# One tower of a vision transformer on one core: the class rows' product through Wo ahead of the third group's turnings, the last tiles normed ahead of low parts, and a token stage and table start in another order

## The chip, the cores and the metric

The kernel runs on one core of a Trainium2 chip. The metric is the device time of one execution in microseconds (us). The core has a matrix engine (TensorE, PE in the profile; PEld is its weight load), VectorE (DVE), ScalarE (ACT), GpSimd (POOL) and SyncE (SP), which run their own instruction streams side by side and wait for each other by counting semaphores. Matmul results lie in eight banks of PSUM.

## The reference

```python
h = ssm_kernel(x, ...)                      # 8 channels x 256 states x 512 lags:
#   z = (1 + dtA/2)/(1 - dtA/2);  K[c,h,l] = 2 Re sum_n Ct[c,h,n] z[h,n]^l,  n < 64
h = concat([cls_tok, h], axis=1)            # 8 x 257 x 512
h = h + attention(layernorm(h))             # 16 heads, q*cos(rot), k*sin(rot), spiral, out @ Wo.T + bo
h = h + moe(layernorm(h))                   # router -> top 2 of 8 experts, gelu(x @ W_e + b_e),
                                            # gates, then @ out_w + out_b
```

All sums have to hold to float32, so the kernel splits each operand of a large product into a high part of fewer bits and a low part, the exact rest, and takes three matmuls instead of one (`split3`).

## The kernel before

**Tables.** The powers z^0 to z^63 of a half (128 states' rows) are made on DVE as products: `low_powers(hf)` makes z^0 to z^15, then `piece(hf, p)` makes 14 pieces of two products each (L1401, L1402): six of upper powers, eight of coefficients with x, one for each channel. A piece goes into one of the slots of `ring` or, later, `r_low`, and can be made only when PE has turned (transposed, L1916) the piece that had the slot. PE turns each piece into two of banks 0 to 3 (`turn_low`, `turn_pieces`), ACT copies them out (`turned`, `keep_pieces`, L955), and when a half is done PE multiplies the tables into token values (`tokens_of_half`, `tokens`), ACT copies these into `so` (`keep_tokens`, L974), and SP and ACT store them and load them back as token tiles. `keep_tokens(n)` for n >= 2 waits until the store of chunk n - 2 is done.

Ahead of this the four weight matrices Wv, Wo, Wq, Wk are turned by PE (`w_turn`), copied as high parts by ACT (`w_high`), reduced on PE by the high part (`w_rest`) and copied as low parts (`w_low`); Wq and Wk are scaled by ACT first (`w_scale`), with factors that POOL makes. Matrix n uses four banks from `W_BANK[n]`. In program order PE does all of this and the class value (L1969) before `turn_low(0)`, which waits for all 16 low parts; ACT has the same order.

DVE makes the squares z^1 to z^256, swaps real and imaginary part with `swapped` (L1311, L1312: -im, re) for z^1 to z^32, makes the low powers, two pieces, the channel powers (`channel_powers`, one semaphore, `dve_power_step`, counts its steps), and then the other pieces. When both halves are done, DVE copies the class row's low part (L1431), takes the statistics of the first two tiles (`ln`, L1417), POOL the power -1/2 (L718), DVE norms them (L1427), PE turns them (L2032).

**Attention** is a loop over eight batches of eight units, the last batch written out with the first routing groups inside it. This loop is not touched. A quad is four token tiles of the second norm: `turn_xn` turns a tile, ACT or DVE copies it (`keep_xnT`), `logits_of(q)` multiplies by the router, ACT copies (`keep_lgT`), `sum_chunks(q)` adds up on PE, DVE takes the logits (`take_logits`, L1541) and the two largest (`top_two`). Quads 0 and 1 are done within attention. Quad 2's tiles are ready by its end; quad 3 has tiles 6 and 7 of both halves, quad 4 the class rows' tile.

**After attention** the order written out is: on PE `project(last, ...)` twice (banks 6 and 7, L2114 and L1969), the turnings of quad 2, the class rows' product through Wo (L2325 and twelve matmuls of L1969, into bank 6, so after the first residual), `logits_of(2)`, then turnings, sums and logits of quads 3 and 4. On DVE: top two of quad 1, low parts of experts 0 and 1 (`lo_expert`, L1713: `ew - ew_hi`, 128x2048), residual and statistics of the first last tile, low part of expert 2, the second tile's, sums, the class tile's residual and statistics, `normalise` of both last tiles (L1508), the class tile's norm (L1742), the logits. POOL adds the output bias to each tile (L803, L826) and takes the powers (L807, L824). ACT makes the experts' high parts (`hi_expert`, L1148) between its copies.

**Routing and tokens.** DVE counts the entries of each expert, gives every entry a slot, and makes one-hot tables (L1783 to L1793). PE multiplies them into tile and place of each slot's token (L2357), DVE turns them into `token_of` (L1804, L1805), and POOL gathers rows by it (L837, 40 tiles of 128 slots; gather i waits for PE to have turned tile i - 2). Each gathered tile is turned by PE (L2133), copied high by ACT (L1163), low by DVE (`lo_xs`, L1746), and multiplied by its expert's matrix (L1969), which DVE's `dve_expert_low` must have reached. The low parts of experts 0 to 2 count one by one, that of expert 6 counts for 3 to 6 together. Then come bias, gelu, store, and at the end gathering, gating and the output matrix.

The queue of SP is in program order too: it stores the last tiles and the class tile when they are normed, and only then loads experts 6 and 7.

## Time and profile before

| | |
|---|---|
| median of 3 runs | 748.42 us (747.17 to 749.06) |
| profiled execution | 749.32 us, of which its instructions span 747.6 |
| busy: PE / PEld / DVE / ACT / POOL | 679.0 (91%) / 543.2 (73%) / 526.1 (70%) / 413.2 (55%) / 151.3 (20%) |
| mean granted TensorE clock | 0.968 of 2.4 GHz |
| HBM | 45.42 MB read, 30.16 MB written |

All times below are microseconds from the span's start in that profiled execution. A timeline row gives start, duration, engine, line, operation, output and inputs, their shapes and how many such instructions are merged (xN); in brackets stands how long the engine was idle before it and what ended that. The clock column is the share of 2.4 GHz that TensorE was granted: 1.00 is the level of 2.4 GHz, 0.50 that of 1.2.

### The profile page before, as it was taken

The page shows a single profiled execution, that of the slowest core. Times are in us where ns is not written, and L with a number is a line of the kernel's source. Part 1 is how long each engine was busy: PE and PEld are TensorE (multiplying, and loading weights), DVE is VectorE, ACT ScalarE, POOL GpSimd, SP SyncE. Part 2 cuts the span into 40 slices and gives each one's busy share as a digit, 9 for nine tenths or more (in the row PEclk, how much of TensorE's full clock was granted, in tenths as well). Part 3 has the DMA queues.
Part 4 walks back from the last instruction along what each step waited for, and adds up shares of the span by engine and source line. Part 5 has one row for each costly group of instructions (what it writes and reads, how often), then busy time and mean ns, then how long its engine had stood idle before and what let it go on. Part 6 is the DMA issues. An engine that isn't in the chain of part 4 may idle for free.

```text
span 747.6 us, 16676 instructions
## 1 busy us (share of the span) xinstructions
PE 679.0 (91%) x5671; PEld 543.2 (73%) x5672; DVE 526.1 (70%) x1211; ACT 413.2 (55%) x1071; POOL 151.3 (20%) x306
## 2 busy tenths in 40 slices
PE   4688887879999999999999999888769999998998
PEld 4477877867778787777878777656448888886786
DVE  7988993556778777787877876678774444445775
ACT  4865544476667677676766766575623333333111
POOL 5200001010121111202112120113032333326560
PEclk9899999989999999999999999999779999999999
DMA  7500356400000010000100004125716765656894
GB/s 208 189 2 15 128 114 147 97 1 1 3 21 37 0 53 3 28 28 14 42 0 28 28 28 145 54 74 208 254 56 195 205 203 169 168 166 203 258 324 175
DMA packets 54553, 76.11 MB, mean 102 GB/s; under 512 B 24666, under 2 KB 26970, under 8 KB 54387
## 3 DMA queue, kind: packets, MB, share of 16 engines
q1 hardware_dynamic: 40850, 42.43, 17.6%
q0 software_dynamic: 5920, 19.40, 9.9%
q10 hardware_dynamic: 7744, 13.77, 5.0%
q8 instruction: 24, 0.39, 0.2%
q14 instruction: 15, 0.11, 0.1%
HBM read 45.42 MB, written 30.16 MB: 101 GB/s over the span
## 4 chain that ended last, share of the span: by engine, by line
PE 74%; DVE 13%; ACT 6%; DMA 3%; issue 2%; POOL 1%; ACTq 0%; DVEq 0%; POOLq 0%
PE ps L1969 45%; PE ps L2072 9%; PE ps L2082 4%; PE ps L2065 4%; PE ps L2133 4%; DVE ring L1401 3%; DVE ring L1402 3%; PE ps L1916 2%; DMA wo_raw<-in_L_attn_Wo_dram 2%; PE ps L2089 1%; ACT prb L1021 1%; DVE ew_lo L1713 1%; ACT pts L1029 1%; PE ps L2032 1%; PE ps L1960 1%
## 5 line engine op out<-in xcount | busy, mean ns | idle before, releaser
L1029 ACT ACTIVATE pts<-ps 128x512 f32<-128x512 f32 x128 | 77.1, 602 | 97.5 <-PE ps L2072 97.4
L1021 ACT ACTIVATE prb<-ps,negmax 128x257 f32<-128x257 f32 x256 | 117.7, 478 | 4.7 <-DVE negmax L1472 3.7
L1472 DVE TENSOR_REDUCE negmax<-ps 128x2 f32<-128x514 f32 x128 | 82.5, 686 | 21.4 <-PE ps L2065 21.4
L2072 PE MATMUL ps<-ident,prb 128*128 128x128 f32 x512 | 83.9, 288 | 6.2 <-ACT pts L1029 3.2
L2072 PEld LDWEIGHTS ps<-ident,prb 128*128 128x128 f32 x512 | 57.3, 144 | 30.7 <-issue 12.0
L1481 DVE TENSOR_SCALAR prb<-prb,rrec 128x258 f32<-128x258 f32 x256 | 73.4, 351 | 2.3
L1203 ACT ACTIVATE rows<-ps 128x512 f32<-128x512 f32 x40 | 23.9, 598 | 84.7 <-DVE ps L1826 82.7
L1969 PE MATMUL ps<-ew_hi,xnT_hi 128*128 x160 | 67.0, 419 | 0.1
L1969 PE MATMUL ps<-ew_lo,xnT_hi 128*128 x160 | 63.4, 396 | 0.0
L1969 PE MATMUL ps<-ew_hi,xnT_lo 128*128 x160 | 63.1, 394 | 0.0
L1746 DVE TENSOR_TENSOR xnT_lo<-ps,xnT_hi 128x512 fp32r<-128x512 f32 x40 | 27.7, 691 | 49.6 <-ACT xnT_hi L1163 31.1
L837 POOL DMA_INDIRECT rows<-xn_dram,token_of x40 | 40.2, 1006 | 109.9 <-PE ps L2133 85.7
L1021 ACT ACTIVATION_READ_ACCUMULATOR prb<-ps,negmax 128x1 f32 x256 | 53.8, 210 | 0.0
L1916 PE MATMUL ps<-ident,ring 128*128 128x128 f32 x384 | 46.4, 275 | 7.0 <-DVE ring L1402 6.1
L1916 PEld LDWEIGHTS ps<-ident,ring 128*128 128x128 f32 x384 | 41.8, 141 | 11.3 <-DVE ring L1402 10.1
L1478 DVE RECIPROCAL rrec<-rowsum 128x4 f32<-128x4 f32 x64 | 11.4, 178 | 53.6 <-ACT prb L1021 53.3
L1826 DVE TENSOR_TENSOR ps<-ps,eb 128x512 f32<-128x512 f32 x40 | 28.0, 699 | 23.0 <-PE ps L1969 22.9
L2133 PE MATMUL ps<-ident,rows 128*128 128x128 f32 x228 | 34.8, 276 | 7.1 <-DMA rows<-xn_dram,token_of 4.1
L760 POOL TENSOR_TENSOR pcls<-prb,ones 128x12 f32<-128x12 f32 x40 | 8.6, 215 | 155.3 <-DVE prb L1481 155.3
L2133 PEld LDWEIGHTS ps<-ident,rows 128*128 128x128 f32 x228 | 28.2, 141 | 15.9 <-issue 4.9
L1969 PE MATMUL ps<-xT_hi,wqT_hi 128*128 128x258 f32 x128 | 39.0, 305 | 0.0
L1969 PE MATMUL ps<-xT_hi,wkT_hi 128*128 128x258 f32 x128 | 38.7, 303 | 0.0
(402 smaller groups left out, 1772.5 us busy)
## 6 DMA issues: line engine op xcount, KB each, us to landing
y_slots<-rows ACTq DMA_DIRECT2D x40, 256.0 KB
ew<-in_L_ffn_expert_w_dram SPq DMA_DIRECT2D x8, 1024.0 KB, 9.0
h_dram<-h_ob SPq DMA_DIRECT2D x17, 256.0 KB, 2.0
xn_dram<-tok SPq DMA_DIRECT2D x17, 256.0 KB, 2.2
h_late<-h_dram SPq DMA_DIRECT2D x12, 256.0 KB
out_dram<-h_late SPq DMA_DIRECT2D x11, 256.0 KB
y_slots<-u_sb SPq DMA_DIRECT2D x9, 256.0 KB, 5.8
tok_dram<-so SPq DMA_DIRECT2D x4, 512.0 KB, 3.2
```

What stands on the lines that cost most here:

```text
L837: pool.indirect_dma_start(out=rows[:, i % 2, :], out_offset=None, in_=xn_dram, in_offset=bass.IndirectOffsetOnAxis(ap=token_of[:, i:i + 1] ...
L1021: e = act.activation(prb[:, u % 2, j, 0:KEYS], ps[:, j, 0:KEYS], ACT.Exp, bias=negmax[:, u % 2, j:j + 1], accum_out=rowsum[:, u % 2, j:j + 1])
L1029: act.activation(pts[:, slot:slot + 2, :, st * P:(st + 1) * P], ps[:, 4, :].rearrange("p (h t s) -> p h t s", h=2, t=HALVES), ACT.Copy).th ...
L1472: dve.tensor_reduce(negmax[:, u % 2, 2 * b:2 * b + 2], ps[:, 2 * b:2 * b + 2, 0:KEYS], AX_X, ALU.max, negate=True).then_inc(s["dve_max"], 1)
L1481: e = dve.tensor_scalar(prb[:, u % 2, j, :], prb[:, u % 2, j, :], rrec[:, u % 2, j:j + 1], None, ALU.mult)
L1826: dve.tensor_tensor(ps[:, u, :], ps[:, u, :], eb[:, e, :], ALU.add).then_inc(s["dve_bias_added"], 1)
L1916: mm = pe.matmul(ps[:, n % 4, q * P:(q + 1) * P], part(q), ident[:, :], is_transpose=True, start=(k == 0 and q == 0), stop=(k == len(parts ...
L1969: mm = pe.matmul(out_ap, a, b, start=start and i == 0, stop=stop and i == 2, skip_group_check=skip)
L2065: mm = pe.matmul(ps[:, j, 0:KPAD], a[rows, ci, st * P:(st + 1) * P], b[rows, ci, :], start=(a is q_hi and b is k_hi), stop=(b is k_lo))
L2072: mm = pe.transpose(ps[:, 4, (2 * j + tt) * P:(2 * j + tt + 1) * P], prb[:, u % 2, 2 * b + j, tt * P:(tt + 1) * P], ident[:, :])
L2082: mm = pe.matmul(ps[j * DH:(j + 1) * DH, 5, 0:KEYS], v_sb[:, tt, h * DH:(h + 1) * DH], pts[:, h, tt, 0:KEYS], start=(tt == 0), stop=(tt == ...
L2133: mm = pe.transpose(ps[:, bank, k * P:(k + 1) * P], src[:, k * P:(k + 1) * P], ident[:, :])
```

## The change

On ACT, PE and DVE instructions change their places; the values computed stay the same.

- ACT swaps z^1 to z^32 into `zt` (two copies of 128x768 behind Wv's low parts), and DVE waits for them (`act_params` counts two more everywhere).
- PE turns z^0 to z^15 right after the class value, then Wq, piece 0, Wq's rest, piece 1, Wk, Wk's rest. Wk moves from banks 0 to 3 to banks 4 to 7, behind Wq's low parts (`W_AFTER`). ACT has the matching order.
- The scratch of `low_powers(1)` lies in slot 0 instead of 1, so it waits for piece 12 of half 0, not 13.
- ACT copies half 1's low powers ahead of token chunk 2, and piece 0 ahead of chunk 3.
- The copy of the class row's low part goes behind the first norm.
- After attention: the class rows' product ahead of quad 2's turnings; on DVE residuals, statistics and norms first, with expert 0's low part in two halves between, expert 1's after the class tile's statistics, expert 2's in the token stage; on ACT `hi_ot` ahead of `hi_expert(0)`, and the high parts of experts 2, 3 each one place later.
- `token_of` is computed right after the one-hot tables instead of after seven further small steps.

```diff
@@ -84,9 +84,11 @@
-    W_BANK = (4, 0, 4, 0)
+    W_BANK = (4, 0, 4, 4)
+    W_AFTER = {2: 0, 3: 2}
-    CHANNELS_DONE = POWERS_DONE + 36
+    TABLE_POWERS_DONE = 3 * 5
+    CHANNELS_DONE = POWERS_DONE + 34
@@ -884,6 +886,9 @@
+            act.wait_ge(s["dve_power_step"], TABLE_POWERS_DONE)
+            act.activation(zt[:, 0:NZ - 1, :, 0, :], zs[:, 0:NZ - 1, :, 1, :], ACT.Copy, scale=-1.0).then_inc(s["act_params"], 1)
+            act.activation(zt[:, 0:NZ - 1, :, 1, :], zs[:, 0:NZ - 1, :, 0, :], ACT.Copy).then_inc(s["act_params"], 1)
@@ -895,24 +900,13 @@
-            act.wait_ge(s["act_params"], 3)
+            act.wait_ge(s["act_params"], 5)
-            act.wait_ge(s["loaded_wk"], 16)
-            act.wait_ge(s["pool_angles"], 4)
-            w_scale(wk_raw, k_scale)
-            w_high(2, wqT_hi)
-            w_low(2, wqT_lo)
-            act.activation(bvc_hi[:, :], bv_col[:, :], ACT.Copy).then_inc(s["act_bias_high"], 1)
-            w_high(3, wkT_hi)
-            w_low(3, wkT_lo)
-            act.wait_ge(s["act_bias_high"], 1)
-            act.activation(bvc_neg[:, :], bvc_hi[:, :].bitcast(F32), ACT.Copy, scale=-1.0).then_inc(s["act_bias_high"], 1)
-
@@ -981,16 +975,30 @@
-            keep_pieces(0, 0, 2)
+            act.wait_ge(s["loaded_wk"], 16)
+            act.wait_ge(s["pool_angles"], 4)
+            w_scale(wk_raw, k_scale)
+            w_high(2, wqT_hi)
+            keep_pieces(0, 0, 1)
+            w_low(2, wqT_lo)
+            act.activation(bvc_hi[:, :], bv_col[:, :], ACT.Copy).then_inc(s["act_bias_high"], 1)
+            keep_pieces(0, 1, 2)
+            w_high(3, wkT_hi)
+            w_low(3, wkT_lo)
+            act.wait_ge(s["act_bias_high"], 1)
+            act.activation(bvc_neg[:, :], bvc_hi[:, :].bitcast(F32), ACT.Copy, scale=-1.0).then_inc(s["act_bias_high"], 1)
-            keep_tokens(0, 1, 2, 3)
+            keep_tokens(0, 1)
-            keep_pieces(1, 0, upper + GROUP)
+            keep_tokens(2)
+            keep_pieces(1, 0, 1)
+            keep_tokens(3)
+            keep_pieces(1, 1, upper + GROUP)
@@ -1152,11 +1160,10 @@
+            hi_ot(last, 3)
-            hi_ot(last, 3)
-            hi_expert(2)
@@ -1167,9 +1174,10 @@
-                    hi_expert(3)
+                    hi_expert(2)
+            hi_expert(3)
@@ -1311,8 +1319,7 @@
-            swapped(zt[:, 0:NZ - 1], zs[:, 0:NZ - 1])
-            settle()
+            dve.wait_ge(s["act_params"], 4)
@@ -1338,7 +1345,7 @@
-                dve.wait_ge(s["act_params"], 5)
+                dve.wait_ge(s["act_params"], 7)
@@ -1359,7 +1366,7 @@
-                    dve.wait_ge(s["pe_table_turned"], max(turned_before(1, p) for p in (1, upper + 2)))
+                    dve.wait_ge(s["pe_table_turned"], max(turned_before(1, p) for p in (0, upper + 2)))
@@ -1367,7 +1374,7 @@
-                    tmp = ring[:, 1, 0, 0:n]
+                    tmp = ring[:, 1 - hf, 0, 0:n]
@@ -1391,7 +1398,7 @@
-                        dve.wait_ge(s["act_params"], 7)
+                        dve.wait_ge(s["act_params"], 9)
@@ -1427,14 +1434,14 @@
-            dve.wait_ge(s["act_xT_high"], 1)
-            dve.tensor_copy(xT_lo[:, :, BODY:KPAD], xc_lo[:, :, :].bitcast(F32)).then_inc(s["dve_xT_low"], 1)
+            dve.wait_ge(s["act_xT_high"], 1)
+            dve.tensor_copy(xT_lo[:, :, BODY:KPAD], xc_lo[:, :, :].bitcast(F32)).then_inc(s["dve_xT_low"], 1)
@@ -1708,23 +1715,27 @@
+            def lo_chunks(e, k0, k1):
+                dve.wait_ge(s["act_expert_high"], e + 1)
+                return dve.tensor_tensor(ew_lo[:, e, k0:k1, :], ew[:, e, k0:k1, :], ew_hi[:, e, k0:k1, :].bitcast(F32),
+                                         ALU.subtract)
+
-                dve.wait_ge(s["act_expert_high"], e + 1)
-                dve.tensor_tensor(ew_lo[:, e, :, :], ew[:, e, :, :], ew_hi[:, e, :, :].bitcast(F32), ALU.subtract
-                                  ).then_inc(s["dve_expert_low"], done)
+                lo_chunks(e, 0, KC).then_inc(s["dve_expert_low"], done)
-            for e in range(2):
-                lo_expert(e)
-            lo_expert(2)
+            lo_chunks(0, 0, KC // 2)
+            lo_chunks(0, KC // 2, KC).then_inc(s["dve_expert_low"], 1)
+            for st in range(HALVES):
+                normalise(last, st)
@@ -1735,8 +1746,7 @@
-            for st in range(HALVES):
-                normalise(last, st)
+            lo_expert(1)
@@ -1792,6 +1802,12 @@
+            dve.wait_ge(s["pe_token_of"], 1)
+            then(dve.tensor_copy(token_tile[:, :], ps[:, 2, 0:SLOTS]))
+            dve.scalar_tensor_tensor(out=token_of[:, :], in0=token_tile[:, :], scalar=float(P),
+                                     in1=ps[:, 2, SLOTS:2 * SLOTS], op0=ALU.mult, op1=ALU.add
+                                     ).then_inc(s["dve_token_of"], 1)
+
@@ -1800,21 +1816,14 @@
-            dve.wait_ge(s["pe_token_of"], 1)
-            then(dve.tensor_copy(token_tile[:, :], ps[:, 2, 0:SLOTS]))
-            dve.scalar_tensor_tensor(out=token_of[:, :], in0=token_tile[:, :], scalar=float(P),
-                                     in1=ps[:, 2, SLOTS:2 * SLOTS], op0=ALU.mult, op1=ALU.add
-                                     ).then_inc(s["dve_token_of"], 1)
-
-            e = LOWS_IN_ATTENTION + 1
-            dve.tensor_tensor(ew_lo[:, e, 2:KC, :], ew[:, e, 2:KC, :], ew_hi[:, e, 2:KC, :].bitcast(F32), ALU.subtract)
-            dve.wait_ge(s["act_expert_high"], e + 2)
-            dve.tensor_tensor(ew_lo[:, e + 1, :, :], ew[:, e + 1, :, :], ew_hi[:, e + 1, :, :].bitcast(F32), ALU.subtract)
+            lo_expert(2)
+            lo_chunks(LOWS_IN_ATTENTION + 1, KC // 2, KC)
+            lo_chunks(LOWS_IN_ATTENTION + 2, 0, KC)
@@ -1891,7 +1900,7 @@
-                        pe.wait_ge(s["act_w_low"], (n - 2) * KC + ic + 1)
+                        pe.wait_ge(s["act_w_low"], W_AFTER[n] * KC + ic + 1)
@@ -1991,9 +2000,13 @@
+            pe.wait_ge(s["act_w_low"], 2 * KC)
+            turn_low(0)
+            turn_pieces(0, 0, 1)
+            turn_pieces(0, 1, 2)
@@ -2017,9 +2030,8 @@
+            turn_pieces(0, 2, PIECES)
-            turn_low(0)
-            turn_pieces(0, 0, PIECES)
@@ -2318,8 +2330,6 @@
-            for n in range(4 * EARLY_QUADS, 4 * EARLY_QUADS + 4):
-                turn_xn(n)
@@ -2327,6 +2337,8 @@
+            for n in range(4 * EARLY_QUADS, 4 * EARLY_QUADS + 4):
+                turn_xn(n)

```

## Rows read from the trace of the kernel before

**Rows 1.** The page's chain that ended last, shares by engine

```profile
PE 74%; DVE 13%; ACT 6%; DMA 3%; issue 2%; POOL 1%; ACTq 0%; DVEq 0%; POOLq 0%
```

**Rows 2.** DVE's timeline in the tables: start, us, line, operation, idle before and releaser

```profile
17.36 0.56 DVE L1311 TENSOR_SCALAR zt<-zs 128x768 f32<-128x768 f32 x1
...
18.43 0.43 DVE L1319 TENSOR_TENSOR zs<-zs 128x256 f32<-128x256 f32 x1
...
44.90 1.23 DVE L1401 TENSOR_TENSOR ring<-r_low,zs 128x1024 f32<-128x1024 f32 x1 [2.34 <-PE ps L1916]
...
71.01 1.23 DVE L1402 TENSOR_TENSOR ring<-x_in,w_pow 128x1024 f32<-128x1024 f32 x1
```

**Rows 3.** ACT's timeline in the tables

```profile
26.15 2.56 ACT L882 ACTIVATE wq_raw<-wq_raw,q_scale 128x512 f32<-128x512 f32 x4 [1.93 <-POOL k_scale L710]
...
37.36 2.00 ACT L878 ACTIVATE wkT_lo<-ps 128x512 fp32r<-128x512 f32 x4
```

**Rows 4.** PE's timeline, tables and first norm

```profile
39.41 3.63 PE L1916 MATMUL ps<-ident,r_low 128*128 128x128 f32 x16 [1.41 <-ACT wkT_lo L878]
...
85.48 3.68 PE L1916 MATMUL ps<-ident,ring 128*128 128x128 f32 x32 [0.95 <-ACT rT L955]
...
125.38 1.12 PE L2032 MATMUL ps<-ident,xhat 128*128 128x128 f32 x8 [1.74 <-DVE xhat L1427]
```

**Rows 5.** DVE's timeline, second half of the tables and first norm

```profile
74.34 0.11 DVE L1363 MEMSET r_low<- 128x64 f32 x1 [2.10 <-PE ps L1916]
...
87.46 1.23 DVE L1401 TENSOR_TENSOR ring<-r_low,zs 128x1024 f32<-128x1024 f32 x1 [1.22 <-PE ps L1916]
...
122.02 1.29 DVE L1417 BATCH_NORM_STATS2 lnst<-tok 128x6 f32<-128x512 f32 x2
```

**Rows 6.** DVE's timeline after attention

```profile
507.90 4.49 DVE L1713 TENSOR_TENSOR ew_lo<-ew,ew_hi 128x2048 fp32r<-128x2048 f32 x2
...
513.64 2.88 DVE L1713 TENSOR_TENSOR ew_lo<-ew,ew_hi 128x2048 fp32r<-128x2048 f32 x1
...
520.14 1.00 DVE L1508 TENSOR_SCALAR tok<-tok,mv,rs 128x512 f32<-128x512 f32 x2
...
522.57 0.55 DVE L1742 TENSOR_SCALAR tok<-tok,mvc,rsc 128x512 f32<-128x512 f32 x1 [1.43 <-POOL h_ob L826]
...
528.34 0.19 DVE L1541 TENSOR_TENSOR logits<-ps,rb 128x32 f32<-128x32 f32 x1 [2.80 <-PE ps L2176]
```

**Rows 7.** PE's timeline after attention

```profile
510.50 1.91 PE L2133 MATMUL ps<-ident,tok 128*128 128x128 f32 x16
...
520.75 1.97 PE L2133 MATMUL ps<-ident,tok 128*128 128x128 f32 x8 [2.42 <-DVE tok L1508]
```

**Rows 8.** Stretches: us, busy PE, PEld, DVE, ACT, POOL; granted clock; DMA share, GB/s

```profile
513.10:516.00 2.90, 2.86 (x13) 1.34 (x13) 2.90 (x2) 1.90 (x2) 1.27 (x1) 1.00 0.26 97
...
520.70:522.60 1.90, 1.85 (x10) 1.85 (x10) 0.47 (x2) 0.60 (x1) 1.90 (x4) 0.52 0.58 217
```

**Rows 9.** The loads of half 1's tokens, line L532

```profile
L532 SPq DMA_DIRECT2D tok<-tok_dram x4: 383/692/883, 118.2 to 120.1; - x4
...
DMA to landing us min/median/max: 3.2/4.2/4.5
```

**Rows 10.** ACT's timeline after attention

```profile
528.83 1.90 ACT L1148 ACTIVATE ew_hi<-ew 128x2048 fp32r<-128x2048 f32 x1
```

**Rows 11.** POOL's second gather, and line L837's 40 gathers (ns min/median/max)

```profile
548.26 2.91 POOL L837 DMA_INDIRECT rows<-xn_dram,token_of  x1 [0.30 <-issue]
...
L837 POOL DMA_INDIRECT rows<-xn_dram,token_of x40: 944/944/2907, 546.7 to 672.3; - x40
```

**Rows 12.** PE's timeline, last place products

```profile
544.41 0.65 PE L2357 MATMUL ps<-of_tile,of_place 128*128 128x80 bf16 x10 [0.94 <-DVE of_place L1793]
```

**Rows 13.** DVE's timeline, token stage

```profile
545.98 0.19 DVE L1804 COPY token_tile<-ps 128x40 f32<-128x40 f32 x1
...
551.75 0.69 DVE L1746 TENSOR_TENSOR xnT_lo<-ps,xnT_hi 128x512 fp32r<-128x512 f32 x1 [1.43 <-ACT xnT_hi L1163]
```

## The prediction

> **What bounds the kernel now.** I read the page's chain of work first: TensorE (PE) carries three quarters of it and VectorE (DVE) 13% [rows 1]. So a few microseconds won on DVE count only where the chain lies on DVE, or where PE waits for it. There are two such stretches: the building of the tables (0 to 125 us) and the passage from attention to the experts (507 to 555 us). Next I read each engine's timeline there and looked at the idle time in brackets and its releaser.
>
> In the tables DVE works without a pause until 42.56, idles 2.34 us because its ring slot is not yet turned, then runs 24 products up to 72.25, each starting 1.14 us after the last [rows 2]. PE could not turn: it waited for the last low part of Wk [rows 3, 4]. The reader should see a queue, not a shortage of PE: the turnings stand behind four weight matrices in program order. At the half's change DVE idles 2.10 us, then 1.22 us [rows 5], and PE itself idles 0.95 us for a ScalarE (ACT) copy [rows 4].
>
> Behind attention DVE makes low parts of three experts, 2.25 us each, before it norms the last two tiles at 520.14 [rows 6]; PE idles 2.42 us for those and goes on at half clock [rows 7, 8]. DVE then waits 2.80 us for PE's sums at 528.34 and paces the routing.
>
> **The start of the tables.** The two instructions that swap the powers go from DVE to ACT. They cost 18.43 - 17.36 = 1.07 us [rows 2]. On ACT they stand after Wv's low parts, start at about 14.8, and take about 1.6 us (768 columns; ACT's 512 take 0.5 and I scale by columns), so they are done at 16.4, before DVE asks at 17.36. They push Wo's first two copies by half a microsecond, which the pace of PE's turnings behind them absorbs. Without that cover DVE would wait.
>
> PE now turns z^0 to z^15 right after the class value, at about 26.2 (27.2 before, less 1.07, when the powers are ready). ACT: Wq scaled to 28.6, class row 29.1, four table copies to 31.1, Wk scaled (2.5, as Wq [rows 3]) to 33.6, Wq high to 35.5, piece 0 to 36.5, Wq low to 38.4, piece 1 to 39.5, Wk high to 41.4, Wk low to 43.4, then the two channel swaps of 0.95 to 45.4. That uses 0.48 us a copy [rows 3]. PE runs between these: Wq turned at 33, piece 0 at 35 to 36, piece 1 at 38, Wk at 40, its rest at 41.8. DVE finishes the channel powers at 42.56 - 1.07 = 41.49 and finds slot 0 free for five microseconds. Piece 3 at 43.8 needs piece 1 turned (38), piece 4 at 46.0 needs piece 2 turned: ready 43.8, turned 45.8. That is the tightest point, 0.2 us. The whole idle time goes: 44.90 - 41.49 = **3.41 us**. From there the half is DVE's own pace. If piece 0's copies or Wk came 2 us later than I count, the stall would return in part; at worst only the swap's 1.07 us remains.
>
> **The change of halves.** DVE begins z^0 to z^15 of half 1 one turning earlier: its scratch lies in the other slot. That takes away the 2.10 us [rows 5] but does not make the path shorter, for PE must finish the tokens of half 0 and turn the powers before it turns piece 0. What shortens the path is ACT's new order: two token chunks are stored after the low copies. PE's 0.95 us wait goes [rows 4]; DVE then idles about 2.4 us for PE where it idled 1.22. The new waits on a chunk's store stand behind these copies, when the store has had seven microseconds; loads of half its size land in 4.5 at most [rows 9]. **0.95 us**; bounds 0 and 1.22, the idle that DVE has there.
>
> **The first norm.** The copy of the class row's low part no longer stands ahead of the statistics, which start at 122.02 [rows 5]. The tokens' load is the next thing late: it was issued at 118.2, the fastest of its kind lands in 3.2 [rows 9], so the statistics cannot start before 121.4. PE waits 1.74 us for this chain at 125.38 [rows 4], so what is won is PE's: 0.06 to 0.6, I take **0.4 us**.
>
> **After attention.** ACT takes the last high part of the output before an expert's: this wins 0.4 us for DVE's small steps, hidden, as the first residual waits for PE's projection (507.7). DVE in the new order: residual 0 and statistics to 509.05, half a low part (1.14) to 510.2, residual 1 (the projection is done at 510.7, where PE's next turnings follow it [rows 7]) to 511.4, statistics and sums to 512.8, half a low part to 513.9, norming of both tiles to 515.5 at the latest. PE: the class product follows the projection at once, as its bank is free since 508.4: 13 matmuls, 3.0 us [rows 8], 510.7 to 513.7. Then the third group's 16 turnings, 1.9 [rows 7], to 515.5; ACT's last copy at 516.2; its logits to 517.25; turnings of the seventh tiles to 518.3. Here PE waited until 520.75. Now the last two tiles have been ready for three microseconds: turned 519.35. ACT's expert copy between (1.9 [rows 10]) puts the logits' copy at 518.6 and the last of four tile copies at 520.6, so the fourth group's logits are done at 521.7.
>
> The class tile decides next. Product added 516.1, statistics to 517.3, then DVE starts a whole low part, up to 519.5. GpSimd (POOL) took 2.4 us for its power and bias row, from DVE's last statistic at 520.2 to the norming at 522.57 [rows 6]: that gives the class tile at 520.3 if POOL is free. It won't be: the gather at 548.26 took 2.91 us where others take 0.94 and ended 0.85 us after DVE's two-operand low part, and DVE's own low part at 513.64 took 2.88 beside POOL's bias addition where two others took 4.49 together [rows 6, 11]. So I let the power start at 519.5: norming 521.9, turned 522.8, third sums at 523.7. DVE took those logits at 528.34: **4.6 us**; 5.1 us with POOL free.
>
> The Trainium skill ("SBUF — State Buffer", Who interferes with whom) says that a DVE instruction with two SBUF inputs contends with a GpSimd instruction that reads SBUF. By that rule the sum takes 4.6, without it 5.1. The rows agree; the page's inference that descriptor generation escapes this is contradicted by the 2.91.
>
> The experts' high parts 3 and 4 now stand after the loop on ACT: done at 527.8, while PE asks for them at 528.2. The SP queue moves along: both tile stores by 515.5, class stores and the loads of experts 6 and 7 at about 522.3 instead of 523.5. ACT asks for expert 6 some 2.6 us earlier than before, so it may wait for that load; the slot copy behind it is wanted by PE at 536.2, and ACT would have it at 533.2 if it need not wait.
>
> **The token stage.** DVE computes the slots' tokens before seven small steps. PE ends the place products at 545.06 [rows 12]; DVE read them at 545.98 [rows 13]. The gathers start 0.85 us earlier and the second no longer meets a low part. But next late is DVE: before, 3.4 us of low parts ended at 551.75 - 1.43 = 550.32; now they begin 0.85 later (DVE idles for PE, the steps follow) and are 2.24 us longer, since expert 2's stands here: end 553.4, first tile's low part 554.05, and expert product 0 at 554.1 instead of 554.73. **0.5 us**; bounds 0 (a gather holds DVE back) and 0.85.
>
> **Sum.** 3.4 + 0.95 + 0.4 + 4.6 + 0.5 = 9.85 us. The profiled execution took 749.32 (span 747.6), so 739.45; the median of the runs is 0.9 lower: 748.42 - 9.85 = 738.6. Attention's loop and the slots' loop keep their instructions and only shift.
>
> **Rivals.**
> *PE's clock stays low after attention.* Before, PE fell to 1.2 GHz (0.52) after its idle 2.42 us [rows 7, 8]; now it idles 0.9 and twice some 0.4 us. If it falls all the same, the path from the last tiles' turning to the third sums takes what it took, from 520.75 until DVE's 528.34, and now starts at 518.3: the term is 2.4, the sum 7.7, the time 740.7. The shorter idle speaks against it. The Trainium skill ("TensorE: Matmul & The Clock Gate", What's actually happening) has the clock drop where PE was idle before; a price there too would be the 2.2.
> *ACT's queue in the tables is too long.* Piece 2 or 4 is late and DVE stalls again. With 2.3 us lost there the sum is 7.5: 740.9. For it: 0.2 us of slack, and PE at half clock at 39.41, where 16 turnings took 3.63 [rows 4]. Against it: it would cost once, as the pace afterwards is 2.27 for DVE against 1.9 for PE.
> *The tail is hidden.* If ACT's waits for experts 6 and 7, or the low parts ahead of the first tile, pace the passage, the tail gives about 2 us: sum 6.8, time 741.6.
> *Slower.* The slots' loop falls into another rhythm, each gather landing after PE wants it. POOL spends 0.94 us on nearly each of the 40 gathers [rows 11], and PE releases the next one. Forty tiles: from 0.25 us a tile it eats the 9.85; at 0.35 the time is 752. A gather has two tiles of time, so this needs landings over 2 us later, and nothing there is touched.
> *Nothing happens*, the two stretches being covered elsewhere: 748.4; the chain runs through both, so I hardly believe it.
>
> **Chances.** Forecast (within 1.5 us of the sum) 50%; low clock 12%; ACT's queue 14%; hidden tail 15%; slower 4%; nothing 3%; the rest, 2%, is more gain than counted (POOL free, 0.85 in the token stage: 737). The range reaches from 736.3 (all upper bounds: 12.1) to 742.5, which takes in each faster rival alone. A measurement tells about 0.3%, 2.2 us: faster 0.93, same 0.03, slower 0.04.
>
> **What would show it.** DVE without idle time between 17 and 68.8; its first product after the channel powers at 41.5; table pieces of half 1 resuming at 83.1; PE's first norm turning near 120.6. In the tail, measured from the end of the attention loop: no low clock between 513 and 524, logits taken 4.6 us earlier, the class tile about 1 us earlier than before, second gather back to about 1 us, and a DVE busy up to the first slot tile. The prediction is wrong if DVE still waits for the ring in the tables, if PE's wait behind attention only moves to the class tile beyond 522, or if the logits of the last groups are taken no earlier.

## The result and the profile after

The changed kernel took 742.49 us (median of five, 741.86 to 744.39), the kernel before 748.42 beside it: ratio 0.994 (0.9912 to 0.9968). In a second session it took 742.93, ratio 0.9936 (0.9913 to 0.9958). By the medians it is faster by 5.9 us in the first session and by 4.3 in the second; 9.85 were forecast. The traced execution took 743.89 us, its span 742.0 against 747.6.

One thing has to be known first. In each of the later sessions the kernel before ran 17 to 30 times, and these runs lie between 741.9 and 752.2 us. A trace shows one draw from such a spread, and all terms of the forecast were read from one trace.

The page's chain by engine, to be held against [rows 1]: PE has less of it and DVE more, 18% against 13%.

```profile
PE 70%; DVE 18%; ACT 4%; issue 3%; DMA 3%; POOL 1%; ACTq 0%; DVEq 0%; POOLq 0%; SPq 0%
```

DVE's timeline in the tables, of the changed kernel, answers to [rows 2, 5]:

```profile
41.55 1.23 DVE L1408 TENSOR_TENSOR ring<-r_low,zs 128x1024 f32<-128x1024 f32 x1
...
47.26 1.23 DVE L1408 TENSOR_TENSOR ring<-r_low,zs 128x1024 f32<-128x1024 f32 x1 [1.07 <-PE ps L1925]
...
70.02 0.11 DVE L1370 MEMSET r_low<- 128x64 f32 x1
...
84.49 1.23 DVE L1408 TENSOR_TENSOR ring<-r_low,zs 128x1024 f32<-128x1024 f32 x1 [2.58 <-PE ps L1925]
...
118.58 1.29 DVE L1424 BATCH_NORM_STATS2 lnst<-tok 128x6 f32<-128x512 f32 x2 [3.25 <-DMA tok<-tok_dram]
```

The first product comes at 41.55 (41.49 forecast), and the 2.10 us at the half's change are gone. But DVE waits 1.07 us at 47.26. PE's timeline says why (answers to [rows 4]):

```profile
43.97 5.38 PE L1925 MATMUL ps<-ident,ring 128*128 128x128 f32 x32 [3.17 <-DVE ring L1409]
...
121.94 1.11 PE L2044 MATMUL ps<-ident,xhat 128*128 128x128 f32 x8 [1.10 <-DVE xhat L1434]
...
124.01 1.99 PE L1969 MATMUL ps<-rT,lT 128*32 128x64 f32 x126 [0.73 <-issue]
...
128.02 0.39 PE L1978 MATMUL ps<-xT_lo,wqT_hi 128*128 128x258 f32 x1 [1.59 <-issue]
```

PE now stands idle for 3.17 us ahead of the third piece, its granted clock falls to 1.2 GHz, and 32 turnings take 5.38 us, where 16 take 1.97 at 2.4 GHz. The last two rows show pauses for which PE waited on nothing; the kernel before had the second (1.57), not the first.

After attention, DVE's timeline answers to [rows 6]. The window's granted clock follows [rows 8]:

```profile
512.82 1.00 DVE L1515 TENSOR_SCALAR tok<-tok,mv,rs 128x512 f32<-128x512 f32 x2 [0.67 <-POOL rs L809]
...
515.46 2.28 DVE L1720 TENSOR_TENSOR ew_lo<-ew,ew_hi 128x2048 fp32r<-128x2048 f32 x1
519.64 0.55 DVE L1752 TENSOR_SCALAR tok<-tok,mvc,rsc 128x512 f32<-128x512 f32 x1 [1.89 <-POOL h_ob L828]
```

```profile
505.00:524.00 19.00, 15.59 (x108) 10.73 (x106) 15.21 (x56) 10.98 (x15) 8.73 (x8) 1.00 0.61 216
```

The last tiles are normed 7.3 us earlier, PE stays at 2.4 GHz throughout, and the fourth group's logits are taken at 521.80 in place of 528.34. The changed kernel came into this stretch 1.86 us early (the last projection begins at 505.61 in place of 507.47) and leaves it 6.54 us early: 4.68 us, with 4.6 forecast.

The token stage, DVE's and PE's timelines (answers to [rows 12, 13]) and the granted clock at the first expert product:

```profile
538.64 0.20 DVE L1806 COPY token_tile<-ps 128x40 f32<-128x40 f32 x1 [0.94 <-PE ps L2369]
...
541.29 5.62 DVE L1720 TENSOR_TENSOR ew_lo<-ew,ew_hi 128x2048 fp32r<-128x2048 f32 x3
546.83 1.28 DVE L1756 TENSOR_TENSOR xnT_lo<-ps,xnT_hi 128x512 fp32r<-128x512 f32 x2
```

```profile
537.75 0.85 PE L2369 MATMUL ps<-of_tile,of_place 128*128 128x80 bf16 x10 [0.68 <-DVE of_place L1803]
...
547.76 0.79 PE L1978 MATMUL ps<-ew_hi,xnT_hi 128*128 x1 [2.45 <-DVE xnT_lo L1756]
```

```profile
536.00:540.00 4.00, 2.96 (x21) 2.00 (x21) 2.95 (x7) 0.38 (x1) 0.62 (x1) 0.50 0.00 0
...
548.00:552.00 4.00, 4.00 (x10) 3.13 (x11) 4.00 (x3) 0.00 (x0) 0.00 (x0) 0.50 0.23 66
```

DVE ends three low parts at 546.9 and the first tile's behind them, and PE waits 2.45 us for it (before it waited 2.52 us for a gather one step earlier). That product then runs wholly at 1.2 GHz: 5.45 us against 4.68. In two repeats of the kernel before, below, it took 5.15 and 3.94, so this price varies with the clock there too. A little later the chain of waits holds a row that was not in it before, between the second product and the fifth:

```profile
556.87 0.26 issue
557.13 5.74 DMA rows<-xn_dram,token_of
562.87 0.04 issue
562.91 0.66 PE ps L2145 x4
563.57 0.40 issue
563.96 3.03 PE ps L1978 x12
```

A gather ordered at 557.13 is what PE waits for last there. Two slots' starts here are 3.47 and 3.92 us after the ones before, where 3.20 is the rule: about 1 us.

### The profile page after: what moved, and what is told of

It reads as the page before. It is cut to its first block, busy times and chain, and to the rows that moved or that the text cites. A ratio compares the mean times of both kernels' runs of the same rounds, so it can differ in the third digit from the quotient of the medians.

```text
span 742.0 us, 16679 instructions
## 1 busy us (share of the span) xinstructions
PE 676.3 (91%) x5671; PEld 539.3 (73%) x5672; DVE 525.3 (71%) x1210; ACT 413.0 (56%) x1073; POOL 153.2 (21%) x306
## 4 chain that ended last, share of the span: by engine, by line
PE 70%; DVE 18%; ACT 4%; issue 3%; DMA 3%; POOL 1%; ACTq 0%; DVEq 0%; POOLq 0%; SPq 0%
PE ps L1978 44%; PE ps L2084 8%; PE ps L2094 4%; PE ps L2077 4%; PE ps L2145 3%; DVE ring L1408 3%; DVE ring L1409 3%; PE ps L1925 1%; ACT prb L1029 1%; PE ps L2101 1%; PE ps L1956 1%; ACT pts L1037 1%; PE ps L1969 1%; DVE ew_lo L1720 1%; PE ps L2044 1%
## 5 line engine op out<-in xcount | busy, mean ns | idle before, releaser
L1925 PE MATMUL ps<-ident,ring 128*128 128x128 f32 x384 | 48.0, 281 | 8.2 <-DVE ring L1409 8.2
L1925 PEld LDWEIGHTS ps<-ident,ring 128*128 128x128 f32 x384 | 43.5, 144 | 12.2 <-DVE ring L1409 12.0
L1835 DVE TENSOR_TENSOR ps<-ps,eb 128x512 f32<-128x512 f32 x40 | 28.0, 700 | 25.1 <-PE ps L1978 25.1
L2145 PE MATMUL ps<-ident,rows 128*128 128x128 f32 x228 | 34.4, 273 | 4.3 <-DVE rows L1874 3.1
L853 POOL DMA_INDIRECT y_rows<-y_slots,slot_of x34 | 34.4, 1012 | 18.9 <-DVE rows L1874 10.0
```

The lines of the kernel that those rows point to most:

```text
L853: pool.indirect_dma_start(out=y_rows[:, t % Y_RING, k, :], out_offset=None, in_=y_slots, in_offset=bass.IndirectOffsetOnAxis(ap=slot_of[:, ...
L1925: mm = pe.matmul(ps[:, n % 4, q * P:(q + 1) * P], part(q), ident[:, :], is_transpose=True, start=(k == 0 and q == 0), stop=(k == len(parts ...
L2145: mm = pe.transpose(ps[:, bank, k * P:(k + 1) * P], src[:, k * P:(k + 1) * P], ident[:, :])
```

## Marks from all traces

The experiments gave many traces, so the lead can be followed by means. "Low" is the start of the second half's low powers on DVE, "norm" the second statistic of the first norm, "c0", "c1", "c7" PE's first q product of chunks 0, 1 and 7, "logits" DVE's last logits, "tokens" the tokens' numbers, "slot 9" PE's turning of the ninth slot tile. All in us.

```
                    low   norm     c0     c1     c7  logits  tokens  slot 9
old start
before            74.34 122.63 128.46 173.14 438.81  529.65  546.20  578.77
before_again_1    72.04 121.27 127.05 172.28 437.98  528.74  545.27  578.03
before_again_2    74.09 122.94 128.76 172.08 437.81  527.26  543.79  576.35
tail_alone        73.58 122.23 127.95 171.06 436.86  524.55  540.12  573.92
tail_again        75.28 123.49 129.32 172.86 438.49  526.21  541.75  575.92
mean              73.87 122.51 128.31 172.28 437.99
new start
front_alone       70.07 119.44 125.67 172.52 438.44  532.42  548.97  581.72
front_padded      69.87 119.36 125.73 168.86 434.68  527.12  543.67  576.37
front_pad1        68.84 118.61 124.98 168.43 434.32  525.64  542.18  574.78
front_pad3        70.12 119.46 125.82 172.38 438.19  528.82  545.36  578.27
after             70.02 119.19 125.93 170.90 436.86  523.11  538.87  573.22
after_again       68.85 118.11 124.62 169.62 435.38  521.63  537.30  571.47
class_first       68.83 118.48 124.73 169.69 435.47  521.51  537.17  571.46
lows_later        70.13 119.31 125.83 170.32 436.29  522.50  538.06  570.07
mean              69.59 119.00 125.41 170.34 436.20
```

The start's lead is 4.3 us at the half's change, 3.5 at the first norm, 2.9 at chunk 0 and 1.9 at chunk 1, where single traces spread over 4 us. From c1 to c7 every trace of the table takes 265.6 to 266.0 us. All of the spread of the attention stage is made in chunk 0.

before_filled and front_filled, below, have the old and the new tables unchanged; their edits lie in chunk 0. Their low, norm and c0 are 72.03, 120.73, 127.00 and 70.18, 119.76, 126.32. With them the three leads are 3.9, 3.1 and 2.6 us.

Two more marks divide the start as the forecast did: the end of DVE's products of half 0 has a mean of 71.76 with the old start and 69.63 with the new one, and the place where the pieces of half 1 resume (84.49 and 87.46 in the first pair of traces) 87.27 and 84.20. These are leads of 2.1 and 3.1 us.

## The experiments

"Start" is all up to and with the first norm, "tail" the changes after attention and in the token stage.

**The two parts alone.** front_alone is the kernel before with the start's hunks, tail_alone with the tail's.

> The changes up to and with the first norm, on the kernel before; the rest as before. Theory (the profile after taken at its word): the statistics of the first norm start 3.4 us earlier than before (118.6 against 122.0), but the lead is down to about 1.9 us at the last projection (505.6 against 507.5), because the clock falls ahead of the third piece's turning and two short pauses of TensorE come up; from there on nothing is changed, so the end is 1.9 us earlier: about 746.5 us, ratio 0.9975. Rival 1 (the terms of the prediction): 3.4 + 0.95 + 0.4 = 4.75 us, 743.7 us, ratio 0.9937. Rival 2 (the loss inside the attention stage, from 2.4 to 1.9 us, is chance of one execution): the lead at the last projection differs from 1.9 us by over 0.3 us here.

> The changes after attention and in the token stage alone, the start as before. Theory: the last top two of the quads start 4.7 us earlier (523.7 against 528.3), place tiles 0.4 us more, then 0.8 us go back at the first expert product (PE's clock low all through it: 5.45 against 4.68 us), and 0.7 to 1.0 us at the fourth or fifth slot, whose gather lands late beside the first load of ow and a store: an end 3.3 to 4.3 us earlier, 744.1 to 745.1 us, ratio 0.995. Rival 1 (the terms of the prediction): 5.1 us, 743.3 us. Rival 2 (the late gather belongs to one execution only): no pause at the fifth slot here, 4.3 us earlier.

The start alone: ratio 1.000 (0.998 to 1.0019), 12 runs. The tail alone: 0.9949 (0.9922 to 0.9977). The start, early by 3 us at the norm, measured no gain where 0.9975 was expected; the tail came out at the 0.995 that was expected. The start's lead at the end of attention could not be read from one trace: chunk 0 took 46.85 us in front_alone and 43.11 in tail_alone. Both expectations rested on one trace's marks, as the forecast had.

**The changed kernel again.**

> The changed kernel as it is, timed and traced once more, since single executions of the kernels so far spread over 8 us. Theory (a part of each execution is the luck of where TensorE's slow stretches fall): the work before the attention stage keeps its marks within 0.3 us (first norm's statistics 119.2, first turning of x 121.9), while the stretch from the first norm to the end of the first chunk (44.97 us from the first q product of chunk 0 to that of chunk 1 in the profiled execution) differs by 1 to 2 us, chunks 1 to 6 stay at 44.28 us each, and the pause at the fifth slot (lead lost 1.0 us) is there or not. Median 742 to 744.5, ratio 0.992 to 0.996. Rival (the marks are fixed, the spread lies outside of the span): every mark within 0.3 us of the first trace.

The marks of the start moved by 1.2 us, more than expected; chunk 0 took 45.00 us, as in the first trace; the fifth slot's late gather did not show as a wait on the DMA, but the same two slots took 0.7 us too long.

**PE kept busy ahead of the third piece**, in the changed kernel (warm_tables) and in front_alone (front_warm):

```
+ pe.wait_ge(s["act_table_kept"], 8)
+ for _ in range(6):
+     pe.matmul(ps[:, 3, :], nident[:, :], wkT_hi[:, 0, :], start=True, stop=True, skip_group_check=True)
  turn_pieces(0, 2, PIECES)
```

> The changed kernel with six idle 128x512 products (their bank is overwritten and not read) in TensorE's pause of 3.17 us ahead of the third piece's turnings. Theory: TensorE keeps its full clock, the 16 turnings of a piece take 1.9 us in place of 3.3, VectorE's wait of 1.07 us behind them falls to under 0.2, and everything up to the first norm is 1.0 to 1.1 us earlier: first norm's statistics at 117.5 in place of 118.6, end at best 1.1 us earlier than the changed kernel. Rival: the piece's turnings are slow for another reason (two passes of a cold bank or of the copies), and the wait stays at 1 us or more: same marks as the changed kernel within 0.2 us.

> The start's changes on the kernel before, with six idle products that keep TensorE busy in its pause ahead of the third piece. The start alone measured no gain (ratio 1.000, 0.998 to 1.0019) although its first norm was 3.2 us early. Theory A (the lead is real and was lost to slow stretches of TensorE, of which some are luck): with the fall at the third piece gone, the first turning of x is 3.4 us early, and the end is 2 to 3.5 us earlier than before: 745 to 746.5 us, ratio 0.9955 to 0.9975. Theory B (a lead won before the first norm is given back in the first chunk whatever it is, since something there ends at its own time): ratio 0.9985 to 1.001, and the first q product of chunk 1 within 1 us of the kernel before's 173.1.

PE's timeline of warm_tables:

```profile
41.35 1.56 PE L2035 MATMUL ps<-wkT_hi,nident 128*128 128x512 f32 x6
43.99 1.97 PE L1925 MATMUL ps<-ident,ring 128*128 128x128 f32 x16 [1.08 <-DVE ring L1409]
46.26 1.97 PE L1925 MATMUL ps<-ident,ring 128*128 128x128 f32 x16 [0.30 <-DVE ring L1409]
```

A piece takes 1.97 us and DVE never waits there; low powers at 68.88. The clock was the cause of the 1.07 us. after_again and class_first stand at 68.85 without idle products: there PE came late from Wk, idled 1.20 and 1.23 us ahead of the third piece, kept 2.4 GHz, and DVE did not wait. In lows_warm, below, PE came to the six products only at 43.48, turned the third piece at 44.88, and DVE waited 0.66 us; so they can also stand in the way. In warm_tables the first norm moved by 0.1 us only, since its token load landed 4.58 us after its order in place of 3.12; after_again, with the same low powers, has the norm 1.1 us earlier than the first trace. warm_tables' ratio, 0.9917 (0.9887 to 0.9947), is not apart from the changed kernel's. front_warm came out slower than before: 1.0022 (1.0004 to 1.0041). So theory A fell, and theory B with it, since its chunk 1 began at 167.12: a kernel whose trace stood 5.7 us ahead of the first trace's at chunk 7 was 1.8 us slower in the median. The traced execution took 746.31 us, 2.7 less than that median, so one trace says little here; but something behind attention had to be looked at.

**A pause on DVE.** DVE's timeline of front_alone, and below it that of front_pad1 (see below). Column two is the duration, here of two norms together:

```profile
521.30 0.17 DVE L1743 TENSOR_SCALAR rsc<-mvc 128x2 f32<-128x2 f32 x1
521.75 2.30 DVE L1515 TENSOR_SCALAR tok<-tok,mv,rs 128x512 f32<-128x512 f32 x2 [0.27 <-issue]
```

```profile
515.61 0.17 DVE L1744 TENSOR_SCALAR rsc<-mvc 128x2 f32<-128x2 f32 x1
515.69 1.00 DVE L1516 TENSOR_SCALAR tok<-tok,mv,rs 128x512 f32<-128x512 f32 x2
```

In front_alone the norms start 0.45 us after the last statistic, waiting for nothing, where it is 0.08 in the kernel before (the statistic at 520.06, the norms at 520.14 [rows 6]). So the second one meets POOL's sum for h, and it takes 1.84 us in place of 0.54. POOL's timeline of front_alone:

```profile
522.20 1.26 POOL L828 TENSOR_TENSOR h_ob<-tok,ob 128x512 f32<-128x512 f32 x1
```

This was so in all four traces with the new start, the old tail and no more instructions for DVE, and in none of five with the old start and tail (before_filled and before_warm, below, among them). From that statistic to the last logits the four took 11.1 to 11.6 us, the others 10.2, 9.6, 9.5, 9.4 and 6.8. DVE's code before this place is one instruction shorter with the new start (two swaps and a wait became one wait). Three kernels were to give it back:

```
front_padded:  dve.wait_ge(s["act_params"], 4)      written twice
front_pad1:    dve.memset(lnr[:, 0, :], 1.0)        one memset of lnr
               dve.memset(lnr[:, 1, :], 1.0)        split into two
front_pad3:    the same memset split into four
```

> The start's changes on the kernel before, with one wait of VectorE written twice, so that VectorE's stream from there on has as many instructions as in the kernel before (the start's changes took one out). In both traces with the start's changes VectorE stood 0.43 us after the class tile's last statistic without waiting for anything (0.06 us before), its second norm then fell beside GpSimd's sum for h and took 1.84 in place of 0.54 us, and the last logits lost 1.1 us. Theory (the pause sits at a place in VectorE's code): here the norm starts within 0.1 us, takes 0.54 us, and the stretch from the first k product of the last chunk to the last logits is 1.1 to 1.4 us shorter than with the start's changes alone (92.6 to 94.0 us there, of which 0 to 1.5 by the clock). End 1 us earlier. Rival (the pause comes with the time or with GpSimd's work, not the place): it is there again.

> The start's changes on the kernel before, with VectorE's setting of lnr to one (in its wait ahead of the first norm) split into two instructions, so that its code behind that has as many instructions as the kernel before has. Theory (the pause belongs to a place in VectorE's code, counted in instructions): the norm starts within 0.1 us of the class tile's last statistic, the second norm takes 0.54 us, the stretch from the last chunk's first q product to the last logits 89.5 to 91.5 us, and the end is 1.5 to 2 us earlier than with the start's changes alone: ratio 0.998. Rival (it belongs to what stands before it, not to the place): 0.43 and 1.84 us again, ratio 1.000.

> The same with three instructions more in place of one. By the theory of places the pause has moved ahead by two more instructions and is not at the norms either (it is met by an earlier instruction of the same stretch, where it costs 0.4 us or nothing): 0.54 us for the second norm, ratio 0.998. By the rival 0.43 and 1.84 us again.

In front_padded the doubled wait left no instruction in the trace, so it is front_alone once more: the pause is there, 2.31 us for the two norms, ratio 1.0016 (0.9994 to 1.0038). In front_pad1 and front_pad3 it is gone: 1.00 us for both norms, 10.0 and 9.3 us to the last logits, ratios 0.9974 (0.9957 to 0.999) and 0.9975 (0.9952 to 0.9998). One memset split in two, in a place where DVE waits anyway, is worth some 2 us, and the start alone is worth 1.9 us (0.2 to 3.6 by the intervals), not nothing. The four kernels with the pause measured 1.000, 1.0016, 1.0008 (front_filled, below) and 1.0022.

**Luck of the clock in the old start.** before_filled and front_filled have ten idle products in chunk 0, five ahead of the last k's low part and five ahead of the class value's; before_warm has 17, ahead of the turnings of Wo, of Wq and of the low powers. The first five, as an example; the others have the same form, those ahead of Wo without a wait:

```
  if u == 1 and first:
+     pe.wait_ge(s["dve_qk_low"], 2 * KC - 2)
+     for _ in range(5):
+         pe.matmul(ps[:, 5, :], nident[:, :], wkT_hi[:, 0, :], start=True, stop=True, skip_group_check=True)
      pe.wait_ge(s["dve_qk_low"], 2 * KC)
```

> The kernel before with ten idle 128x512 products in the first chunk (five while the last k of chunk 0 is awaited, five while the class value's high part is). Theory: TensorE's slow stretches near 145 and 159 us go, 1 to 3 us of the first chunk with them: 43 us or less from the first q product of chunk 0 to that of chunk 1 in place of 44.7, end 1 to 2.5 us earlier than before, ratio 0.9965 to 0.9985. Rival: the slow stretches come from the waits near 165 us as well and only move: same as before.

> The start's changes with the same ten idle products. Theory A (the lead of the start, 3.2 us at the first norm, is only hidden by the luck of slow stretches in the first chunk and costs 1.1 us at VectorE's pause after attention): 1.5 to 2.5 us earlier than the kernel before with the same products, ratio of the two 0.997 to 0.998. Theory B (something else takes the lead back always): no difference between the two with an interval of 1.5 us.

> The kernel before, traced once more. Theory 1 (luck in the first trace): the turning of the low powers starts between 36 and 39.5 us (36.3, 37.0 and 39.4 in the three traces with the old start so far), VectorE's wait behind it is anywhere from 0 to 2.4 us, and the second half's low powers start near 72 to 74 us. Rival 2: they are as in the first trace, 39.4, 2.34 and 74.3 within 0.3 us.

> The kernel before, traced a third time; as for before_again_1. With both, the mean start of the first norm's statistics with the old start is expected at 121.5 to 122 us, 2.4 to 2.9 us behind the 119.1 that the traces with the new start show, in place of 3.4.

> The changes after attention and in the token stage alone, traced once more: an old start, for the same comparison, and a second look at the tail: from the first k product of chunk 7 to the last logits 86.2 us where no slow stretch falls near 496 us and 87.7 where one does (90.8 with the old tail), and 15.6 us from there to the token numbers (16.55 with the old one).

> The kernel before with 17 idle 128x512 products in TensorE's waits ahead of the turnings of Wo, of Wq and of the low powers. Theory 1: with TensorE at its full clock the old order has little to wait for: the low powers' turning starts at 36 to 36.5 us and takes 2.0 us, VectorE does not wait at the table's start (0 to 0.4 us), the second half's low powers start at 71.5 to 72.3 us, with no edit of the order; the end about 1 us earlier than before, ratio 0.997 to 1.000. Rival: the order itself costs the 2.3 us; the wait is still over 1.5 us.

before_filled measured 0.9994 (0.9971 to 1.0017), front_filled 1.0008 (0.9986 to 1.003): chunk 0 took 43.8 and 43.9 us, nothing won that can be told, and front_filled had DVE's pause. In the three new traces the old start's low powers were turned at 36.3, 39.4 and 40.7 us. The wait of 2.34 us on which the forecast rested was 0, 2.06 and 3.29 in them, and 0 in tail_alone, where DVE waited 1.43 us two pieces later. PE's timelines of before_again_1 and before_again_2:

```profile
14.97 1.97 PE L1898 MATMUL ps<-ident,wo_raw 128*128 128x128 f32 x16 [1.69 <-DMA wo_raw<-in_L_attn_Wo_dram]
...
36.30 3.57 PE L1916 MATMUL ps<-ident,r_low 128*128 128x128 f32 x16 [1.41 <-ACT wkT_lo L878]
```

```profile
15.24 3.50 PE L1898 MATMUL ps<-ident,wo_raw 128*128 128x128 f32 x16 [1.86 <-DMA wo_raw<-in_L_attn_Wo_dram]
...
39.43 3.36 PE L1916 MATMUL ps<-ident,r_low 128*128 128x128 f32 x16 [1.41 <-ACT wkT_lo L878]
```

One program, and its low powers are turned 3.1 us apart: Wo's turnings ran at 2.4 GHz in one and mostly at 1.2 in the other, and all matrices queue behind them. The other four traces of the old start agree: where Wo took 1.97 us (tail_alone, before_filled) the low powers were turned at 36.3 and 37.0, where it took 3.15 and 3.21 (before, tail_again) at 39.4 and 40.7. But the first trace was no freak. The five old starts of the table have their norm at 121.3 to 123.5, mean 122.5 (122.2 with before_filled); the expectation of 121.5 to 122 missed, and theory 1 holds for single traces only. tail_again met its own expectation: 87.7 us from c7 to the last logits and 15.5 from there to the tokens' numbers. before_warm had no wait at the table's start, low powers at 72.04 and the norm at 120.12: with a fast clock the old order is 1.1 us behind the new one's mean of 119.0 there (118.5 to 120.1 in the kernels with idle products in the tables and the new start). By these marks most of what the new order wins is that it suffers less from the clock. before_warm's ratio was 0.9982 (0.9954 to 1.001).

**The class tile's power** (class_first):

```
- lo_expert(1)
  dve.wait_ge(s["pool_rstd"], NB + 1)
  ...
  dve.tensor_scalar(tok[:, CLS, :], tok[:, CLS, :], mvc[:, 0:1], rsc[:, 1, 0:1], ALU.subtract, ALU.mult
                    ).then_inc(s["dve_xn"], 1)
+ lo_expert(1)
```

> The changed kernel with the whole low part of expert 1 moved from before the class tile's norm to behind it. Theory: GpSimd's power of the class tile takes 2.66 us because the low part runs beside it on VectorE; without it 0.7 us, the class tile's norm starts at 517.3 to 517.6 in place of 519.6, the low part fills VectorE's pause ahead of the last logits, and those start at about 519.5 in place of 521.8: 2.0 to 2.3 us off, the end about 2 us earlier than the changed kernel (740.5 us, ratio to the kernel before 0.9895). Rival: the power is long by itself (it was 0.70 us in other places) or GpSimd's sum for h is what holds the norm: norm later than 519 and nothing gained, or 1.0 us lost because the low part is now on the path.

POOL's timeline of class_first:

```profile
514.20 0.69 POOL L826 TENSOR_TENSOR rsc<-rsc,mhalf 128x2 f32<-128x2 f32 x1 [2.93 <-DVE rsc L1747]
514.85 1.27 POOL L828 TENSOR_TENSOR h_ob<-tok,ob 128x512 f32<-128x512 f32 x1
```

The power takes 0.69 us in place of 2.66, and against the lead that it came with the norm is 2.0 us earlier. But from c7 to the last logits it took 86.04 us against 86.25: 0.2 won, where 2.0 to 2.3 were expected. The low part now stood ahead of the logits of the third group, and for the fourth ACT was next, which has an expert's high part and four tile copies in one queue (in the changed kernel up to 518.7). Ratio 0.9923 (0.9892 to 0.9954). What the forecast charged for POOL, 0.5 us, cost about 0.2.

**The order of the low parts in the token stage.** lows_later:

```
  lo_expert(2)
  lo_chunks(LOWS_IN_ATTENTION + 1, KC // 2, KC)
- lo_chunks(LOWS_IN_ATTENTION + 2, 0, KC)
  ...
  lo_xs(0, 0)
+ lo_chunks(LOWS_IN_ATTENTION + 2, 0, KC)
  lo_xs(1, 1)
```

lows_warm adds the six idle products of warm_tables. combined adds them too and has:

```
- lo_expert(1)                                        (ahead of the class tile's norm)
- lo_expert(2)
+ lo_expert(1)                                        (behind the gates)
  lo_xs(0, 0)
+ lo_expert(2)
  lo_xs(1, 1)
+ lo_chunks(LOWS_IN_ATTENTION + 1, KC // 2, KC)       (both were ahead of lo_xs(0, 0))
+ lo_chunks(LOWS_IN_ATTENTION + 2, 0, KC)
```

> The changed kernel with the low part of expert 5 (2.25 us of VectorE) moved from ahead of the first slot tile's low part to behind it. Theory (the first expert product waits for VectorE, 2.45 us of PE's idle time): the first expert product starts at 545.3 to 545.6 relative to the changed kernel's marks in place of 547.8, 2.2 us earlier, and so does the end, unless the clock is at its low level for longer: end 1.2 to 2.2 us earlier than the changed kernel. Rival: the gather of the second slot tile or the low parts of experts 6 and 7 end last: the third expert product not earlier by over 0.5 us.

> The changed kernel with three edits: six idle products ahead of the third piece's turnings; the low part of expert 1 moved out of the class tile's norm into the token stage; and there the order low 1, slot tile 0, low 2, slot tile 1, low 4's half, low 5. Theory: 1.0 us at the table; class tile's power 0.70 in place of 2.66 us and the last logits 2.0 us earlier; first expert product 2.0 + 2.4 us earlier, of which the third expert product keeps 2.7 because the low parts on VectorE (9 us of them behind the gates) end last there. Together 3.5 to 4 us: about 738.6 us, ratio 0.987. Rival: VectorE's low parts hold the third expert product where it was, and only the table's 1 us is left: 741 us, ratio 0.990.

> The changed kernel with two edits: the low part of expert 5 behind the first slot tile's low part, and the six idle products ahead of the third piece. Theory: their single effects add, 1.5 to 2.2 us for the first and 1 to 1.5 for the second (against the changed kernel in the same session 1.5 us and, across sessions, 2.3 us): 739 us, ratio to the kernel before 0.987 to 0.990. Rival: no better than each alone, 0.9915.

From the tokens' numbers to slot 9 the kernel before and its two repeats took 32.6 us, the five traces of the table with the new tail and its order 33.8 to 34.4 (mean 34.2), lows_later 32.0, lows_warm 32.0, combined 36.9. The other traces lie closer together: warm_tables, with the new order, took 33.4, and the other eight with the old tail 32.1 to 33.7. By all traces it is 34.0 against 32.8. PE's timelines of lows_later and of combined:

```profile
545.06 0.66 PE L1978 MATMUL ps<-ew_hi,xnT_hi 128*128 x1 [0.52 <-DVE xnT_lo L1756]
```

```profile
559.95 0.49 PE L1978 MATMUL ps<-ew_hi,xnT_hi 128*128 x1 [4.51 <-DVE xnT_lo L1755]
```

In lows_later PE's wait of 2.45 us is 0.52. In combined the low parts end at 557.2, the first bias addition and the third tile's low part queue behind them, and PE waits 4.51 us: 0.9965 (0.9946 to 0.9983), where 0.987 was expected. By its median it is 2.2 us slower than the changed kernel beside it, and the trace shows 2.7 lost up to slot 9. lows_later gave 741.43 us, 0.9917 (0.9896 to 0.9939), where after_again beside it had 0.9936. lows_warm has the lowest ratio, 0.9907 (0.9873 to 0.9941), with a median of 740.63 us; 0.987 to 0.990 was expected. (warm_tables has the lowest median, 740.44, in another session.) Neither is shown to beat the changed kernel, as the intervals overlap.

## Why the prediction was too high

The direction was right, and so were most mechanisms. The sum was 9.85 us, the medians show 4.3 and 5.9. Three steps failed: the size of the start's first term, that attention only shifts, and that the token stage's count could end at the first expert product. Means are those of the table's traces.

- **Start of the tables, 3.4: 2.1 measured.** The order did what was forecast: the stall at 44.90 went, DVE's first product came at 41.55. "From there the half is DVE's own pace" failed. Two things made the term too large. The old stall was a draw: 2.34 in the first trace, 0 to 3.29 and 1.8 us by the mean of the five old starts. And the forecast had piece 2 (the third one) "ready 43.8, turned 45.8", with 0.2 us to spare, at full clock. In the trace PE, relieved of the matrices, idled 3.17 us, fell to 1.2 GHz, and the piece was turned at 47.2; DVE waited 1.07 us, and 0.7 by the mean of the eight new starts. warm_tables shows that cause. The rival on ACT's queue had this stall, with PE at half clock as an argument for it and a price of 2.3 us, but ACT's queue was not late. The clock rival was put after attention, where it did not come.
- **Change of halves, 0.95, and first norm, 0.4: right.** The lead grows from 2.1 us at the end of half 0's products to 3.1 where half 1's pieces resume and 3.5 at the norm. The lead of 4.3 us at DVE's low powers holds 2.1 us of DVE's own wait, which the forecast did not count as won, rightly. Where DVE did not stall, in after_again, all marks came as forecast: low powers at 68.85 (68.8), pieces resumed at 83.41 (83.1), the norm's turning at 120.87 (120.6).
- **"Attention's loop and the slots' loop keep their instructions and only shift."** This step failed. The lead falls from 3.5 to 2.9 us ahead of the loop, by PE's pauses without a wait (a new one of 0.2 to 0.7 us), and to 1.9 in chunk 0. The last 1.0 is within the spread of single traces and may be luck of the clock; which, stays open. Start in all: 1.9 instead of 4.75, and 1.9 is also what front_pad1 and front_pad3 measured at the end.
- **After attention, 4.6: 4.1 measured.** The first pair of traces gave 4.68. From c7 to the last logits the kernel before and its repeats took 90.8, 90.8 and 89.5 us, the changed kernel 86.25 twice, both kernels with the tail alone 87.7. In these two the granted clock was 0.61 and 0.68 between 496 and 500 us, where the changed kernel had 1.00, so their term was 2.6.
- **Token stage, 0.5.** Right up to where the count ended: from the last logits to expert product 0 the kernel before and its repeats took 25.1 us, the new tail 24.5. The failed step is to end the count there, at "expert product 0 at 554.1". From product 0 to slot 9 the old tail took 24.1 us and the new one 25.3. Of these 1.2 us, 0.8 lie in the first product, ahead of which PE now waits 2.45 us and which runs at 1.2 GHz (5.2 us up to the third slot, 4.4 before), and 0.4 in late slots; before_again_2 has a late slot too and warm_tables has none, so that part may be luck. Net -0.6, and -0.3 by all traces. The wait was in the rival of the hidden tail, as "the low parts ahead of the first tile": lows_later, with one low part moved, has product 0 2.0 us earlier after the logits. But from there to slot 9 it still took 25.0.

By these means: 1.9 + 4.1 - 0.6 = 5.4 us, between the two measured differences. That the start alone measured nothing had one more cause, which the changed kernel does not meet since its tail norms elsewhere: DVE's pause, some 2 us. By the marks, start and tail should therefore be worth more together in the changed kernel than each alone; the ratios (0.994 against 1.000 and 0.9949) do not separate this from the spread.

The rival "slower" by the gathers' rhythm did not come: one gather was late, not forty. The range's lower end was mis-added: its upper bounds, 3.41, 1.22, 0.6, 5.1 and 0.85, give 11.2 and not 12.1, so 737.2 and not 736.3 us. This changes nothing in the outcome.

## What to carry to other kernels

Before a wait in one trace is booked as a gain, trace the kernel before two or three times: here the wait behind the first term was 0, 2.1, 2.3 and 3.3 us in traces of one and the same order. When an engine is relieved, ask what its new idle time does to its clock, and whether the lead meets a load, a pause or a queue behind the next stage. Follow a gain past the point where the count ends: here the token stage won 0.5 us up to its first product and lost 1.2 behind it. And where a part alone measures nothing, look for a fixed loss that it shifts onto the path before calling it useless; a mere extra instruction may move it away.

## What was new about the hardware

- An engine pauses at places of its code with no wait shown: DVE for 0.45 in place of 0.08 us ahead of its norms, PE 1.0 to 2.0 us twice between 107 and 132 us in 19 of the 20 traces, once in before_warm. With one or three instructions more ahead of it, DVE's was gone. The page of the profile lists instruction packets on two DMA queues, and in the changed kernel one of 16 KB begins at 107.4 and at 125.2, 1.2 us ahead of PE's pauses at 108.55 and 126.43; that the pauses are loads of code fits, but was not shown.
- The cost of DVE's pause was the meeting with POOL, 1.84 us for a norm of 0.54. This norm reads one tensor. The Trainium skill ("SBUF — State Buffer", Who interferes with whom) says that such an operation can take the port pair that DVE and GpSimd share, and that whoever issues first holds it for the whole instruction; POOL's sum had started 0.01 us before the norm and took 1.26 us, as it does alone, and the trace agrees.
- A power of two columns on POOL takes 0.7 us alone, and 2.66 beside a low part on DVE; the tile that needs it can still be early enough.
- PE's granted clock fell to 1.2 GHz after idle times that look harmless, 3.17 us ahead of the third piece and 1.84 us ahead of the place products, and did not after 1.20 us ahead of the third piece. Where the slow stretches fall differs between executions of one program and moves a stage by 3 us.
